# Attention over the batch: 23 of 128 softmax sums made by TensorE instead of VectorE

## The reference, cut to what matters

```
attn = einsum('brnd,brmd->brnm', q, k)
attn = softmax(attn, axis=0)        # over the batch b, not over m
out  = einsum('brnm,brmd->brnd', attn, v)
```

## Time and profile before

| engine | busy us of the span | busy from 244 to 281 us (one group) |
|---|---|---|
| DVE | 481.1 (80%) | 37.00 of 37 |
| PE | 504.8 (84%) | 28.80 |
| POOL | 387.7 (65%) | 34.45 |
| ACT | 328.3 (55%) | 25.86 |

### The profile page before, as it was taken

How to read it: one execution, slowest core, us unless ns; L and a number is a source line. 1 busy time by engine, 2 the same in 40 slices (tenths; PEclk the granted TensorE clock), 3 DMA queues, 4 the chain that set the end, 5 groups by cost and what they waited for, 6 DMA issues and landing times.

```text
span 598.2 us, 13058 instructions
## 1 busy us (share of the span) xinstructions
PE 504.8 (84%) x4610; PEld 308.1 (52%) x4611; DVE 481.1 (80%) x876; ACT 328.3 (55%) x709; POOL 387.7 (65%) x243
## 2 busy tenths in 40 slices
PE   3999687877877778777777877799999999999996
PEld 1554354444444444444444444468986656656665
DVE  5658967999999999999999999978777873333455
ACT  3624674676676766767667676624433533333341
POOL 3200483999899998999999899923105267766640
PEclk9998895999899999999999899999999999999999
DMA  7130257244243332332433320000013223322276
GB/s 225 37 110 1 85 167 253 81 124 130 78 112 84 94 105 73 112 98 80 106 88 93 96 78 2 2 1 1 2 55 101 71 75 107 99 87 90 83 290 211
DMA packets 34288, 56.62 MB, mean 95 GB/s; under 512 B 8541, under 2 KB 21494, under 8 KB 34102
## 3 DMA queue, kind: packets, MB, share of 16 engines
q1 hardware_dynamic: 28950, 43.95, 24.8%
q0 software_dynamic: 3744, 10.39, 5.6%
q10 hardware_dynamic: 1536, 1.51, 0.8%
HBM read 38.43 MB, written 17.40 MB: 93 GB/s over the span
## 4 chain that ended last, share of the span: by engine, by line
PE 37%; POOL 29%; DVE 17%; issue 10%; ACT 3%; DMA 3%; POOLq 0%; SPq 0%; ACTq 0%; DVEq 0%
POOL e_ring L459 29%; PE ps L1890 12%; PE ps L1911 6%; DVE m_bf L1042 4%; DVE x_hat L1049 4%; PE ps L1693 2%; PE ps L1820 2%; DVE stats L865 2%; PE ps L1879 2%; ACT e_ring L644 1%; PE ps L1900 1%; PE ps L1590 1%; PE ps L1621 1%; PE ps L1839 1%; PE ps L1767 1%
## 5 line engine op out<-in xcount | busy, mean ns | idle before, releaser
L459 POOL TENSOR_TENSOR e_ring<-e_ring,x_hat 128x1024 f32<-128x1024 f32 (+1 forms) x127 | 269.8, 2127 | 30.7 <-ACT x_hat L655 18.5
L644 ACT ACTIVATE e_ring<-ps 128x1024 f32<-128x1024 f32 x128 | 131.1, 1025 | 89.7 <-PE ps L1693 89.5
L1042 DVE TENSOR_REDUCE m_bf<-ps 128x128 bf16<-128x1024 f32 x128 | 154.9, 1211 | 4.2 <-PE ps L1684 4.2
L1049 DVE TENSOR_REDUCE x_hat<-e_ring 128x128 f32<-128x1024 f32 x128 | 154.5, 1207 | 3.2 <-ACT e_ring L644 3.2
L1693 PE MATMUL ps<-m_bf,ident_neg 128*128 128x512 bf16 x256 | 82.2, 404 | 61.7 <-DVE m_bf L1042 61.5
L1712 PE MATMUL ps<-e_ring,v_slot 128*32 128x128 f32 x2048 | 86.5, 286 | 1.1 <-POOL e_ring L459 0.6
L1684 PE MATMUL ps<-q_stack,k_stack 72*128 72x128 bf16 x1024 | 83.4, 227 | 3.9 <-DMA k_stack<-qk_parts 3.9
L1712 PEld LDWEIGHTS ps<-e_ring,v_slot 128*32 128x32 f32 x2048 | 50.4, 110 | 58.0 <-issue 51.1
L1684 PEld LDWEIGHTS ps<-q_stack,k_stack 72*128 72x128 bf16 x1024 | 61.9, 101 | 32.0 <-issue 25.8
L1890 PE MATMUL ps<-w_sb,e_ring 128*128 x156 | 74.0, 598 | 1.3 <-ACT e_ring L744 0.8
L477 POOL DMA_INDIRECT e_ring<-token_rows,slot_x x39 | 37.7, 966 | 43.2 <-DVE slot_y L1331 29.5
(11 more groups left out here) (237 smaller groups left out, 674.2 us busy)
## 6 DMA issues: line engine op xcount, KB each, us to landing
q_stack<-qk_parts SPq DMA_DIRECT2D x32, 288.0 KB
k_stack<-qk_parts SPq DMA_DIRECT2D x32, 288.0 KB
w_sb<-in_w13T_dram SPq DMA_DIRECT2D x16, 256.0 KB, 7.6
qk_parts<-e_ring SPq DMA_DIRECT2D x8, 384.0 KB, 3.4
qk_parts<-scratch SPq DMA_DIRECT2D x2, 1536.0 KB, 19.7
x_res<-in_x_dram SPq DMA_DIRECT2D x8, 256.0 KB, 3.9
w_sb<-in_w2T_dram SPq DMA_DIRECT2D x8, 256.0 KB, 7.5
work<-pair_rows SPq DMA_DIRECT2D x8, 256.0 KB, 4.7
```

The source lines that it names most:

```text
L459: nc.gpsimd.tensor_tensor(ev, ev, view(x_hat, CH + (u % RS) * P, [[0, quads], [1, P], [0, 2]]), ALU.mult).then_inc(norm_done, 1)
L644: nc.scalar.activation(e_ring[:, u % ER, :].rearrange("p (q n k) -> p q n k", q=BQ, k=2), view(ps, 2 * (v % SLOT) * CH, [[2 * P, BQ], [1, ...
L1042: nc.vector.tensor_reduce(m_bf[:, u % 2], view(ps, 2 * (v % SLOT) * CH, [[1, P], [P, B]]), AX, ALU.max).then_inc(max_done, 1)
L1049: nc.vector.tensor_reduce(s_sum[:, u % 2], by_position(e_ring[:, u % ER, :]), AXY, ALU.add).then_inc(sum_done, 1)
```

## The change: what it does

In each group the units u = 0, 8 and 12 (in the last group 0 and 8), 23 of 128, get their sum from PE: eight fp32 matmuls with the identity as weights add the eight images' exponentials up in PSUM bank 7, 128 columns wide. They are spread over four steps, two images a step, in PE's steps U+2 to U+5, between scores and subtract. DVE's `total` is left out for these units. ACT takes the logarithm from bank 7 and does both logarithm and inverse of such a unit at the head of its step U+6 (otherwise at the end of step U+2). POOL and `product` take such a unit as the last of its head: the order in the head is 1, 2, 3, 0 (`TURN`; `PLACE_OF` is a unit's place in it), and `product` still does one place a step, so units 1, 2 and 3 of that head come one step earlier. The waits are counted by place. Two kinds of waits are new on PE: the first two sums of a unit wait for the logarithm of the PE-summed unit before it (bank 7 is free then), at u = 8 also for `add_heads`; and `transpose_heads` waits for the logarithm of the group's unit 0.

```diff
+        def summed_on_pe(U):
+            return U % UPG in ((0, 8) if U // UPG == NG - 1 else (0, 8, 12))
+        def turns(h):
+            return [4 * h + i for i in ((1, 2, 3, 0) if summed_on_pe(4 * h) else (0, 1, 2, 3))]
+        SUM_BANK, SUM_STEPS, SUM_AT = 7, 4, 2
 ...
             def exponentials(U, v, u):
                 act.wait_ge(sub_done, U + 1)
-                if later_than(U, ER):
-                    act.wait_ge(pv_done, U - ER + 1)
+                if U >= ER:
+                    act.wait_ge(pv_done, PLACE_OF[U - ER] + 1)
 ...
+            def logarithm(U):
+                if summed_on_pe(U):
+                    act.wait_ge(pe_sum_done, PE_SUMS.index(U) + 1)
+                    total = ps[:, SUM_BANK, 0:P]
+                else:
+                    act.wait_ge(sum_done, DVE_SUMS.index(U) + 1)
+                    total = s_sum[:, DVE_SUMS.index(U) % 2]
+                nc.scalar.activation(s_ln[:, PLACE_OF[U] % 2], total, ACT.Ln).then_inc(ln_done, 1)
 ...
             def attention_step(U, v, u, g, has):           # ACT
+                late = U - SUM_AT - SUM_STEPS
+                if late >= 0 and late < UNITS and summed_on_pe(late):
+                    logarithm(late)
+                    inverse(late)
                 if has(1):
                     exponentials(U - 1, v - 1, (u - 1) % UPG)
-                if has(2):
-                    logarithm(U - 2, (u - 2) % UPG)
-                    inverse(U - 2, (u - 2) % UPG)
+                if has(2) and not summed_on_pe(U - 2):
+                    logarithm(U - 2)
+                    inverse(U - 2)
 ...
             def attention_step(U, v, u, g, has):           # DVE
                 if has(0):
                     maximum(U, v, u)
-                if has(1):
+                if has(1) and not summed_on_pe(U - 1):
                     total(U - 1, (u - 1) % UPG)
 ...
+            def partial_sum(U, step):                      # PE
+                n = PE_SUMS.index(U)
+                if step == 0:
+                    pe.wait_ge(exp_done, U + 1)
+                    if n >= 1:
+                        pe.wait_ge(ln_done, PLACE_OF[PE_SUMS[n - 1]] + 1)
+                    if U % UPG == 8 and U >= UPG:
+                        pe.wait_ge(x2_added, U // UPG)
+                for b in range(step * (B // SUM_STEPS), (step + 1) * (B // SUM_STEPS)):
+                    last = nc.tensor.matmul(ps[:, SUM_BANK, 0:P], ident[:],
+                                            view(e_ring, (U % ER) * UW + (b // 2) * (2 * P) + b % 2, [[2, P]]),
+                                            start=(b == 0), stop=(b == B - 1))
+                if step == SUM_STEPS - 1:
+                    last.then_inc(pe_sum_done, 1)
 ...
             def attention_step(U, v, u, g, has):           # PE
                 if has(0):
                     scores(U, v, u, g)
+                summed = U - SUM_AT - (U - SUM_AT) % SUM_STEPS
+                if 0 <= summed < UNITS and summed_on_pe(summed):
+                    partial_sum(summed, U - SUM_AT - summed)
                 if has(1):
                     subtract(U - 1, v - 1, (u - 1) % UPG)
                 if has(LAG):
-                    product(U - LAG, (u - LAG) % UPG, g)
+                    product(U - LAG)
```

More of the change, by code:

```diff
@@ L301, in attention_steps @@
                 step(UNITS + u, UNITS + u, u, NG, lambda k: k > u)
+        def summed_on_pe(U):
+            return U % UPG in ((0, 8) if U // UPG == NG - 1 else (0, 8, 12))
+        def turns(h):
+            return [4 * h + i for i in ((1, 2, 3, 0) if summed_on_pe(4 * h) else (0, 1, 2, 3))]
+        TURN = [U for h in range(UNITS // 4) for U in turns(h)]
+        PLACE_OF = {U: p for p, U in enumerate(TURN)}
+        DVE_SUMS = [U for U in range(UNITS) if not summed_on_pe(U)]
+        PE_SUMS = [U for U in range(UNITS) if summed_on_pe(U)]
+        SUM_BANK, SUM_STEPS, SUM_AT = 7, 4, 2
         def score_banks(v):
@@ L454, in _, with weights @@
                                         parts[s // 2][:, s % 2, 1, c * CH:(c + 1) * CH], ALU.subtract).then_inc(part3, 1)
-            def weights(U, u, quads=BQ):
-                pool.wait_ge(r_done, U + 1)
+            def weights(turn, p, u, quads=BQ):
+                pool.wait_ge(r_done, turn + 1)
                 ev = e_ring[:, u % ER, 0:quads * 2 * P]
-                nc.gpsimd.tensor_tensor(ev, ev, view(x_hat, CH + (u % RS) * P, [[0, quads], [1, P], [0, 2]]), ALU.mult
+                nc.gpsimd.tensor_tensor(ev, ev, view(x_hat, CH + (p % RS) * P, [[0, quads], [1, P], [0, 2]]), ALU.mult
                                         ).then_inc(norm_done, 1)
             with pool.Fori(0, NG - 1) as g:
[L463 to L467, removed]
+                for p in range(UPG):
+                    weights(g * UPG + p, p, TURN[p])
+            for p in range(UNITS - UPG, UNITS - 2):
+                weights(p, p, TURN[p])
+            weights(UNITS - 2, UNITS - 2, UNITS - 2, BQ // 2)
             for b in range(B):
@@ L645, in exponentials, with inverse @@
                                      view(ps, 2 * (v % SLOT) * CH, [[2 * P, BQ], [1, P], [P, 2]]), ACT.Exp).then_inc(exp_done, 1)
[L647 to L655, removed]
+            def logarithm(U):
[6 more added lines that the diff above has]
+                nc.scalar.activation(s_ln[:, PLACE_OF[U] % 2], total, ACT.Ln).then_inc(ln_done, 1)
+            def inverse(U):
+                p = PLACE_OF[U]
+                act.wait_ge(ln_done, p + 1)
+                if p >= RS:
+                    act.wait_ge(norm_done, p - RS + 1)
+                nc.scalar.activation(s_inv[:, p % RS], s_ln[:, p % 2], ACT.Exp, scale=-1.0).then_inc(r_done, 1)
             def evacuate(g):
@@ L1046, in total @@
                 dve.wait_ge(exp_done, U + 1)
[L1047 to L1049 removed]
+                n = DVE_SUMS.index(U)
+                if n >= 2:
+                    dve.wait_ge(ln_done, PLACE_OF[DVE_SUMS[n - 2]] + 1)
+                nc.vector.tensor_reduce(s_sum[:, n % 2], by_position(e_ring[:, u % ER, :]), AXY, ALU.add).then_inc(sum_done, 1)
             def normalise_last(U, first):
@@ L1696, in subtract, with product @@
                 last.then_inc(sub_done, 1)
-            def product(U, u, g):
-                i, mh, nh = u // 4, (u // 2) % 2, u % 2
[L1700 to L1705, removed]
+            def partial_sum(U, step):
[12 more added lines that the diff above has]
+                    last.then_inc(pe_sum_done, 1)
+            def product(p):
+                U, grp = TURN[p], p // UPG
+                u = U % UPG
+                i, mh, nh = u // 4, (u // 2) % 2, u % 2
+                if p % 4 == 0:
+                    pe.wait_ge(v_slot_ready[i], grp + 1)
+                if p % UPG == 0 and p >= 1:
+                    pe.wait_ge(acc_out, grp)
+                if U >= UNITS - 2:
                     pe.wait_ge(norm_last, U - UNITS + 3)
@@ L1714, in product @@
                                             view(e_ring, (u % ER) * UW + (b // 2) * (2 * P) + b % 2, [[2, P]]),
-                                            start=(u == 0 and b < 4), stop=(u == UPG - 1), skip_group_check=True)
+                                            start=(p % UPG == 0 and b < 4), stop=(p % UPG == UPG - 1), skip_group_check=True)
                 last.then_inc(pv_done, 1)
@@ L1720, in transpose_heads @@
                 pe.wait_ge(acc_out, group)
+                if group < NG:
+                    pe.wait_ge(ln_done, PLACE_OF[group * UPG] + 1)
                 for nh in range(H):
```

3 lines of the change are left out of this document (2 added, 1 removed).

## The result

The changed kernel takes 609.37 us as the median of four runs (604.22 to 610.21); the kernel before, run beside it, 601.22 (598.89 to 604.62). The ratio is 1.0145, 95% interval 1.0103 to 1.0188: slower by 8 us. The forecast was slower by 1.9, 602.3, range 594 to 609. The sign was right and the size not. The profiled execution took 609.18 us (span 607.2).

A forecast was written before the change was run, and what follows sets the result against it. DVE was taken as the bound, with a loop only 0.44 us to spare. 3.52 - 1.26 - 2.80 - 1.32 = -1.86, slower by 1.9: 602.3 us, range 594 to 609.

The forecast's parts named there:

- seven full groups: Per group, u = 8 gains 0.44 us; u = 12 loses 0.18 and u = 0 loses 0.40, by late subtractions.
- unit 8 of the last group, and the end: Last group: unit 8 gains 0.44 us like every u = 8; POOL's work was taken to fit its steps.
- the first group's unit 0: No logarithm to wait for, but PE at half clock: 1.32 us lost; ends 1.8 lost or 0.44 gained.
- slow stretches that are there anyway: Existing low-clock stretches on PE: 0.37 us each, 0.44 more in a step with sums; not in the sum.
- at nothing: Effects given no cost: ACT's logarithm and inverse at the step's head, POOL's uneven units, units coming earlier, transposes' wait, SP's loads.
- The bound and the loop: DVE bounds at 2.26 us a step; a sum can't start before 2.95 after its maximum, so DVE stalls 0.69.
- PE's wait for bank 7: First sums of u = 12 and u = 0 wait for ACT's logarithm: DVE stalls of 1.31 and 1.53 us.
- The allowance for such errors: Twenty-two places with 0.1 us each, all one way: 2.3 us, giving the forecast's own range 599 to 606.
- TensorE's clock: Rival: fourteen new waits on PE each bring a slow stretch of 0.81 us, 11.3 more, 614 us; chance 0.07.
- The rule on the clock: Short idle times between PE's matmul groups can swing its clock; basis of the 614 us rival, chance 0.07.

The follow-up runs named there:

- sums left out: Changed kernel without the 23 PE sums, their units left undivided and ACT taking the logarithm of a constant 1: 595.33 us, ratio 0.9936.
- Opening the loop: Changed kernel with DVE summing two steps after the maximum, product six steps after scores, PE-summed units' logarithm ahead of the exponentials: 587.05 us, ratio 0.9811.
- 592.4 for 595.2: Changed kernel with PE-summed units' logarithm one step earlier, ahead of the exponentials: 595.17 us; the same with the last group's sums on DVE: 592.38 us.
- The load alone: Kernel before plus four unused fp32 matmul records in the same 92 steps, DVE making all sums: 603.63 us, ratio 1.0043.

## Why the prediction was right in sign and wrong in size

The parts of the sum, as forecast and as found (us, minus is lost):

| part | forecast | found |
|---|---|---|
| seven full groups | 7 x 0.44 - 1.26 - 2.80 = -0.98 | -3.7 |
| unit 8 of the last group, and the end | +0.44 | -1.0 |
| the first group's unit 0 | -1.32 | about 0 |
| slow stretches that are there anyway | at nothing | -4 to -5, what is left of 9 |

- *The bound and the loop*: right. The 2.95 us from maximum to sum makes the stall; forecast 0.69, and without PE's part (sums left out) 0.63 of idle time, which is 0.71 from start to start, as two records of DVE overlap by 0.08 (1.21 long, 1.13 apart). Opening the loop removed it.
- *PE's wait for bank 7*: right in place and cause, **the first step that failed in size**. Counted the same way, the stalls are 0.71, 1.48 and 1.68 instead of 0.69, 1.31 and 1.53. PE went on 0.13 after the logarithm (245.10 against 244.71 + 0.26) and not 0.03, and the first four records took 245.64 - 245.10 = 0.54 and not 0.44; the logarithm was 0.04 shorter. Small errors, but all one way, in fourteen places: a full group lost 0.53 instead of 0.14, seven of them 3.7 instead of 0.98. **This term was 2.7 us too small.** The allowance for such errors, 0.1 in each of 22 places, is 2.2 (the forecast has 2.3), so they alone would have stayed inside its range.
- *The first group's unit 0*: forecast 1.32 lost. From the first maximum to the first addition it was 0.3 to 0.7 more in the changed kernel, and that has the 0.53 of a full group in it: about nothing. In the first profile PE had its full clock back at 100 us, in the second at 106, as in the kernel before. These 1.32 are most of the 1.9 forecast; that they made up for a part of what was missing, and helped the sign, is luck.
- *At nothing: the end.* Missed. Unit 8 is last of its head, POOL waits for it, and then the last seven and a half multiplications run one after the other. In the full clock this is 1.0 us (30.7 with the sums left out against 29.7), and the 0.44 that unit 8 was to gain there isn't felt. Taking the last group's sums back gave more than that (592.4 for 595.2, and 605.1 or 603.3 for 608.4), since a late end also brought slow stretches with it.
- *TensorE's clock*: **the largest step that failed, a term that the sum doesn't have.** The forecast wrote down that a slow stretch costs 0.37 and with sums 0.44 more, used this only for new stretches that the new waits might bring, and put it at nothing for those that are there without any new cause. The new waits brought none, and the old gap goes on bringing them: one of these costs 0.35 to 0.45 in a group of the kernel before and 1.30 in the changed one. The load alone, without loop and waits, brings 0.90 to 0.95. In the last group of the first profile two longer ones cost 4.3 (35.0 against 30.7).
- *The rule on the clock* (the Trainium skill, "TensorE: Matmul & The Clock Gate", section "A second HAM failure mode: psum-queue depth-cycling") says that short and frequent idle times of PE between groups of matmuls made the clock swing between its levels. Over the six groups of the first profile of the changed kernel there is no slow stretch, though PE waited at each of the new places (0.76 and 0.96 in turn). The stretch at 373 began at the 1.10 gap at the addition, in a step without sums. Here the trace doesn't bear the rule out for the new waits; for the old gap it does.

So 3.7 and 1.0 could be read from the profiles, and the remaining 4 to 5 of the 9 us between the medians (608.4 and 599.3) go with the slow clock. How they divide isn't shown: the two profiles of the changed kernel have none and one slow stretch in the six groups, fewer than the three of the kernel before, and what they lost to the clock lies at the end of the attention, in the last part and, in the second, ahead of the first maximum. The time that a run loses to the clock differs between kernels (9.4 to 18.8 us), and the changed kernel was timed in eight runs only. What starts a slow stretch at one addition and not at the next stays open.

## What to carry to other kernels

Work taken off an engine without idle time is worth only what the loop through the other engines leaves. Add up what that engine still does between two instructions of which one depends on the other, and compare it with the time of the way round through the other engines. A new reader of a buffer must be placed early in its engine's order, or the engine that waits for the buffer passes the delay on to everything behind it. And an engine that is filled to nine tenths, or a loop that has nothing to spare, has lost its cover: price the disturbances that are there already (a slow clock, a late transfer) again with the new load, and put them into the sum.

## What the runs showed of the hardware

PE's clock fell at an idle time of 1.10 us, or within 2.2 us behind it, in 16 of 63 cases, and at none of the waits of 0.76 and 0.96 us ahead of the new sums. Filling helped: with eight score matmuls repeated in three of sixteen steps around that gap, the clock stayed full for 281 and 280 us on end in the two profiles taken, and by the medians the time fell by 3.5 and 3.7 us. One profile of the changed kernel without the repeats also had its full clock for 273 us, so a single profile doesn't show it. What speaks for it is that none of 14 additions brought a slow stretch with the repeats, against 16 of 63 without. PE went on 0.13 us after the end of an operation of ACT that it waited for.
